# Statistics one row-maximum sooner on VectorE, and a negated mean for GpSimd's two normalizations

## What is computed

```python
x = x + attn(_layernorm(x), ctx, ctx, lengths)   # 8 heads of 16 channels; softmax(s*log(length) * q.k)
x = x + ffn(_layernorm(x), gate_w, w1, w2, w3)

def _layernorm(x, axis=-1, eps=1e-05):
    m = jnp.mean(x, axis=axis, keepdims=True)
    v = jnp.var(x, axis=axis, keepdims=True)
    return (x - m) / jnp.sqrt(v + eps)

def ffn(x, gate_w, w1, w2, w3):
    probs = softmax(x @ gate_w.T); weights, experts = top_k(probs, 2); weights /= weights.sum()
    per expert: w2 @ (silu(w1 @ x) * (w3 @ x)); the sum of the two chosen, by weight
```

## Time and profile before

| | us |
|---|---|
| median of 3 runs | 1182.57 |
| lowest and highest | 1179.75, 1184.3 |
| the profiled execution | 1178.09 |
| its span, first to last instruction | 1176.6 |

### The profile page before, as it was taken

The page is one execution under the profiler, slowest core; times in us unless marked ns, Lnnn a source line. Parts: engine busy times, 40 slices in busy tenths (PEclk is TensorE's granted clock), DMA queues, the critical chain, the costliest instruction groups (busy, mean ns, idle before and its releaser), DMA issues.

```text
span 1176.6 us, 18912 instructions
## 1 busy us (share of the span) xinstructions
PE 1033.1 (88%) x5098; PEld 413.9 (35%) x5099; DVE 683.4 (58%) x1029; ACT 427.9 (36%) x751; POOL 664.4 (56%) x571
## 2 busy tenths in 40 slices
PE   2889999999999999851899999999999999999970
PEld 0223333333333333211344444444444444444430
DVE  5867777777777777304444545455454554544355
ACT  8267777677777777741111011011111011111110
POOL 6454777777777773232386807528383483800574
PEclk9999999999999999985999999999999999999995
DMA  6575666555556544013687656738577466733678
GB/s 198 161 224 159 185 183 181 173 178 184 177 180 180 182 146 120 31 55 90 176 227 200 189 156 168 208 79 232 156 217 170 121 191 171 206 89 89 155 207 264
DMA packets 212726, 195.84 MB, mean 166 GB/s; under 512 B 137376, under 2 KB 176288, under 8 KB 207264
## 3 DMA queue, kind: packets, MB, share of 16 engines
q1 hardware_dynamic: 197760, 122.26, 40.4%
q0 software_dynamic: 14336, 71.87, 18.5%
q10 hardware_dynamic: 576, 1.05, 0.3%
HBM read 111.48 MB, written 53.00 MB: 140 GB/s over the span
## 4 chain that ended last, share of the span: by engine, by line
PE 73%; DMA 7%; DVE 7%; issue 6%; POOL 4%; ACT 1%; POOLq 1%; SPq 0%; PEldq 0%; DVEq 0%
PE rows L1162 32%; PE heads_out L1162 15%; PE heads_out L1076 7%; PE scores L1063 7%; PE rows L1049 6%; DMA W<-parts_dram 4%; DVE nm L760 4%; POOL z L527 2%; PE misc L1126 2%; PE misc L1103 1%; PE misc L1096 1%; ACT W L642 1%; DVE st L870 1%; PE misc L1118 1%; POOL zsc L526 1%
## 5 line engine op out<-in xcount | busy, mean ns | idle before, releaser
L1162 PE MATMUL rows<-W,U 128*128 (+1 forms) x1776 | 391.0, 380 | 17.8 <-DMA U<-stage 17.1
L760 DVE TENSOR_REDUCE nm<-rows 128x2 f32<-128x1024 f32 x256 | 304.3, 1215 | 100.4 <-PE rows L1049 94.0
L642 ACT ACTIVATE W<-scores 128x512 f32<-128x512 f32 x512 | 283.4, 596 | 135.9 <-PE scores L1063 135.0
L1162 PEld LDWEIGHTS rows<-W,U 128*128 128x128 bf16 x1776 | 174.0, 98 | 228.8 <-issue 21.7
L707 ACT ACTIVATE U<-rows 128x512 f32<-128x512 f32 x78 | 46.4, 597 | 509.2 <-PE rows L1162 497.0
L1162 PE MATMUL heads_out<-W,U 128*128 x888 | 197.7, 379 | 2.2 <-DVE U L889 2.2
L1049 PE MATMUL rows<-W,U 96*128 96x512 bf16 x512 | 148.8, 400 | 49.1 <-DMA W<-parts_dram 29.1
L967 DVE TENSOR_TENSOR U<-rows,U 128x512 bf16<-128x512 f32 x78 | 53.9, 691 | 230.6 <-ACT U L707 226.3
L428 POOL TENSOR_TENSOR W<-U,W 128x2048 bf16<-128x2048 f32 x42 | 171.7, 4088 | 7.7 <-POOL W L427 7.7
L1063 PE MATMUL scores<-U,W 128*128 128x512 bf16 x512 | 168.0, 385 | 5.9 <-ACT W L642 5.2
L427 POOL TENSOR_SCALAR W<-U 128x2048 bf16<-128x2048 f32 x42 | 80.8, 1924 | 146.5 <-PE rows L1162 132.8
(11 more groups left out here) (167 smaller groups left out, 723.8 us busy)
## 6 DMA issues: line engine op xcount, KB each, us to landing
U<-wpack_dram POOLq DMA_DIRECT2D x42, 1024.0 KB, 5.9
parts_dram<-U SPq DMA_DIRECT2D x32, 384.0 KB, 4.2
U<-parts_dram SPq DMA_DIRECT2D x32, 384.0 KB, 4.1
W<-parts_dram SPq DMA_DIRECT2D x32, 384.0 KB, 5.3
stage<-slots_dram SPq DMA_DIRECT2D x39, 257.0 KB, 2.9
expert_out_dram<-U SPq DMA_DIRECT2D x39, 256.0 KB
parts_dram<-U SPq DMA_DIRECT2D x32, 256.0 KB, 4.3
stage<-wpack_dram POOLq DMA_DIRECT2D x12, 512.0 KB, 5.4
```

What stands on the lines that cost most here:

```text
L642: s.activation(probs[:, w % 2, j, kk, :], sc[u % 2][:, :], ACT.Exp) \
L760: v.tensor_reduce(nm[:, bb.parity, 2 * k:2 * k + 2], p1[k % 2][:, :].rearrange("p (c k) -> p c k", c=2), AX_X, ALU.max, negate=True).then_ ...
L1162: ins = m.matmul(bank, part_of(s_part, k), W[:, bass.ds(at_w, 512)], start=(k == 0 and n == 0), stop=(k == n_chunks - 1 and n == 2))
```

## The change

VectorE's input statistics stand behind maximum 4 instead of behind maximum 5 and the reciprocal; maximum 5 and the reciprocal follow them. On GpSimd each of the two normalizations gets one more small instruction (column times -1.0, plus 0.0) that makes the negated mean, issued without a wait between it and the instruction that adds epsilon to the variance (`two`), and the pass over 512 columns adds that column where it subtracted the mean. The other edits write the same maxima in fewer calls and adjust counts.

```diff
+    def two(self, first, second):
+        first.then_inc(self.sem, 1)
+        self.done += 1
+        self.step(second)
...
-                    st.step(g.tensor_scalar(psc[:, 0:1], var, EPS, 1.0, ALU.add, ALU.mult))
+                    st.two(g.tensor_scalar(psc[:, 0:1], var, EPS, 1.0, ALU.add, ALU.mult),
+                           g.tensor_scalar(psc[:, 3:4], mean, -1.0, 0.0, ALU.mult, ALU.add))
...
-                    st.step(g.tensor_scalar(norm[:, :], xres[:, pbt.n, :], mean, psc[:, 2:3], ALU.subtract, ALU.mult))
+                    st.step(g.tensor_scalar(norm[:, :], xres[:, pbt.n, :], psc[:, 3:4], psc[:, 2:3], ALU.add, ALU.mult))
...
-                    st.step(g.tensor_scalar(zsc[:, 0:1], mv2[:, 1:2], EPS, 1.0, ALU.add, ALU.mult))
+                    st.two(g.tensor_scalar(zsc[:, 0:1], mv2[:, 1:2], EPS, 1.0, ALU.add, ALU.mult),
+                           g.tensor_scalar(zsc[:, 2:3], mv2[:, 0:1], -1.0, 0.0, ALU.mult, ALU.add))
                     st.step(g.tensor_tensor(zsc[:, 1:2], zsc[:, 0:1], mhalf[:, :], ALU.pow))
-                    st.step(g.tensor_scalar(z[:, pv.parity, 0:D], us[:, :], mv2[:, 0:1], zsc[:, 1:2], ALU.subtract, ALU.mult))
+                    st.step(g.tensor_scalar(z[:, pv.parity, 0:D], us[:, :], zsc[:, 2:3], zsc[:, 1:2], ALU.add, ALU.mult))
...
-                maxima(range(4, 6))
-                if pv.within(0, B - 1):
-                    dve.wait_ge(S["den_in"], b.n * 16)
-                    if pv.within(1, B - 1):
-                        dve.wait_ge(S["rec_out"], b.n * 16 - 16)
-                    v.reciprocal(rden[:, :], den[:, :]).then_inc(S["rec_ready"], 1)
+                maxima(range(4, 5))
                 lb = b.plus(3)
                 if lb.within(0, B - 1):
...
                     v.bn_aggr(mv1[:, lb.parity, :], st1[:, :]).then_inc(S["st1_ready"], 1)
+                maxima(range(5, 6))
+                if pv.within(0, B - 1):
+                    dve.wait_ge(S["den_in"], b.n * 16)
+                    if pv.within(1, B - 1):
+                        dve.wait_ge(S["rec_out"], b.n * 16 - 16)
+                    v.reciprocal(rden[:, :], den[:, :]).then_inc(S["rec_ready"], 1)
                 maxima(range(6, 8))
```

More of the change, by code:

```diff
@@ L17 @@
 LEAD = 4
-ENGINE_STEPS = {"prep": 8, "keys": 4, "z": 3, "route_a": 3, "route_b": 3}
+ENGINE_STEPS = {"prep": 9, "keys": 4, "z": 4, "route_a": 3, "route_b": 3}
 class Batch:
@@ L849, in slot @@
                     q_steps.end()
-                    v.nop().then_inc(S["prep_steps"], ENGINE_STEPS["prep"] - 3)
+                    v.nop().then_inc(S["prep_steps"], ENGINE_STEPS["prep"] - 4)
                     v.nop().then_inc(S["prep_done"], 1)
@@ L863, in slot @@
                         .then_inc(S["m_ready"], 1)
-                maxima(range(12, 13))
-                maxima(range(13, 14))
+                maxima(range(12, 14))
                 if pv.within(0, B - 1):
@@ L876, in slot @@
                     v.bn_aggr(mv2[:, :], st2[:, :]).then_inc(S["st2_ready"], 1)
-                maxima(range(14, 15))
-                maxima(range(15, 16))
+                maxima(range(14, 16))
                 if b.within(B, B):
```

## The result

The changed kernel takes 1162.98 us in the median of 6 runs (1159.15 to 1166.08), the kernel before 1180.26 in 6. The ratio is 0.9848, with a 95% interval from 0.9824 to 0.9873: by that ratio 17.9 us less (17.3 by the medians), where 11.3 less was forecast. The time lies 1 us under the range's lower end of 1164. The direction was right; the gain was taken too small by 6 to 7 us. Another 2.3 us of the distance to the forecast of 1171.3 come from its base, the median of three runs (1182.57), which six runs put at 1180.26.

A forecast was written before the change was run, and what follows sets the result against it. The prediction saw attention slots as a ring of waits around TensorE. It summed 6 us for VectorE's move, 4 for z and 1.3 at the attention's end: 11.3 off the 1182.57 us median gives 1171.3, range 1164 to 1184.

The forecast's parts named there:

- What bounds the kernel: TensorE fills the experts' half; an attention slot of 29.5 us is a ring of waits with no engine full.
- The three waits named: TensorE's waits in eleven slots: VectorE before rows units 7.4 us, GpSimd's z 2.5 or 6.0, the reload 3.4.
- The statistics fit into the gap, 0.67 to 0.78 us a slot: VectorE's 0.89 us of input statistics fit its 1.87 us idle before maximum 5, saving 0.67 to 0.78 us a slot.
- The reload eats part of it: 6 us instead of 9.4: Over twelve slots, late reloads cancel VectorE's gain in three and halve it in two, leaving 6 us; bounds 3 to 9.4.
- The pass at 0.62 us: GpSimd's 128x512 normalization falls from 2.08 to 0.62 us by adding instead of subtracting; held with modest trust.
- The added instruction 0.13 us: Each added 128x1 GpSimd instruction costs 0.13 us: 0.26 us of GpSimd's slot, 0.13 on the way to z.
- z is worth 4 us, near the products' idle time: z 1.33 us sooner removes TensorE's wait in fourteen slots: 3.2 to 7.7 us, taken as 4.
- The queries sooner are worth nothing directly: Queries come 2.7 us sooner on GpSimd; no direct gain, as the reload waits for scores, only room for GpSimd.
- Rival 3: The reload lands sooner because the weight load leaves before it: 16 us less, 1166 us; chance 0.08.
- rival 2: GpSimd's indirect transfers leave sooner, into the reload's flight, making it late: 7 us slower, 1189 us; chance 0.08.
- Rival 1: GpSimd's pass stays at 2.08 us and its room of 0.52 us a slot limits: 1.2 us less, 1181; chance 0.29.
- The signs named: Profile after: line 534 near 620 ns, z's wait about 13 us at the end, maximum 6 close behind, slot 28.6 us.

The follow-up runs named there:

- the VectorE part alone: Changed kernel with GpSimd's lines back to subtracting the mean, only VectorE's input statistics moved: 1173.97 us against 1179.41 for the kernel before, ratio 0.9965.
- the small load: The VectorE part alone with each of ten weight loads cut from 1024 to 64 columns (0.5 MB to 32 KB): 1172.18 us, ratio 0.9940.
- the twelve forms: Changed kernel with 24 more GpSimd passes of 128x512 behind its last work, twelve operation and operand forms, each twice: one execution, 1196.94 us.
- the GpSimd part alone: Changed kernel with VectorE's lines back in the order of before, both GpSimd passes adding the negated mean: 1171.03 us, ratio 0.9933.
- those at 0.6 and 0.7: Changed kernel with GpSimd's weight load behind the keys' first step, 1167.9 us; and with the queries' pass back to subtracting, 1165.96 us.
- the last kernel above: Changed kernel with VectorE's second statistics behind maximum 14 and z's use one score product later: 1172.19 us, ratio 0.9948.

## Why the prediction was wrong in its size

Step by step:

- **What bounds the kernel**: right. All of the gain is in the slots and at their end, and the experts' half didn't move. The three waits named were the ones that changed.
- **The statistics fit into the gap, 0.67 to 0.78 us a slot**: right, and 0.78 it is (29.02 without the move, 28.24 with it).
- **The reload eats part of it: 6 us instead of 9.4**: the first step that failed. The changed kernel's excess is 0.5 us in eleven slots, so most of what lies between 6 and the upper bound of 9.4 came through. The step held the landing of the reload fixed while GpSimd's work moved. For the VectorE part alone its reasoning holds in part: it brought 4 us, the late reloads took about 3.0 from it (the small load gives them back) and GpSimd's limit 2.3. The reading that maximum 6 starts 1.15 us after maximum 5 is over was 1.07 (296.69 less 294.40 + 1.22); nothing in the sum rests on it.
- **The pass at 0.62 us**: right in the choice between 0.62 and 2.08, and the reason given, the pair's operations, is shown by the twelve forms. It is 0.77 because two columns cost 0.15. The Trainium skill (GPSIMD Engine Reference, section 3.1) gives 1.03 cycles per element for a body with at most two operations and makes no exception for a pair with a subtraction. The estimate made from it, 0.63 us, agrees with the 0.62 us for constants without a subtraction and not with the 1.92 us of the same pass with one.
- **The added instruction 0.13 us**: it is 0.27; the 0.13 was that of two casts. With the 0.15 of the columns z came 1.04 sooner instead of 1.33, which costs 0.3 us at the end of the attention and nothing in the slots.
- **z is worth 4 us, near the products' idle time**: the second step that failed. It is 0.52 us a slot (29.53 to 29.01), 7 us in fourteen, near the 7.7 of the weight loads. This is the term that was off most. The distance between the third and the fourth score product shows why. Before:

```profile
283.49 0.39 PE L1063 MATMUL scores<-U,W 128*128 128x512 bf16 x1
284.18 0.66 PE L1096 MATMUL misc<-ident,z 128*128 128x128 f32 x4 [0.29 <-POOLq L529]
284.67 0.38 PE L1063 MATMUL scores<-U,W 128*128 128x512 bf16 x1
```

and after:

```profile
276.50 0.39 PE L1069 MATMUL scores<-U,W 128*128 128x512 bf16 x1
276.73 0.60 PE L1102 MATMUL misc<-ident,z 128*128 128x128 f32 x4
277.17 0.38 PE L1069 MATMUL scores<-U,W 128*128 128x512 bf16 x1
```

  1.18 us and 0.67: the transposes now start while the product before them is still shown as busy, so the idle time between products (0.29) is less than what the wait cost. Starts are to be compared, not ends.
- **The queries sooner are worth nothing directly**: the third step that failed, and the one that made the two parts together more than their sum. No engine waits for them in the slots, but the weight load stands behind them, and it left 1.6 us sooner by the slot's reciprocal.
- **Rival 3, the reload lands sooner as the weight load leaves before it**: this happened beside the forecast, with its 1166 near the result; it was given 8%. The reason named there was right, its sign wasn't: TensorE's wait for the reload didn't go but grew from 3.4 to 4.3 us, as the forecast had it, with the reload up to 1.2 us sooner. Its 1166 is near in part by luck, as it holds the 4 us for z. The prediction weighed it against rival 2 by a count of neighbours (the indirect transfers enter the flight, the weight load leaves it). In the slot of the earlier trace rows the indirect transfers leave 7.8 us after the reciprocal (7.5 in others) and in the changed kernel 6.4, so 1.1 to 1.4 us sooner and not 2.7, and little came late: rival 2 did not happen.
- **Rival 1's account of GpSimd's room** was right where it applies: with slow passes and the statistics moved, GpSimd is the limit at 28.91 us.
- **The signs named**: the slot is 28.24 us and not 28.6; the other signs came as said (the wait for z at the end 13.51 us, maximum 6 close behind maximum 5, line 534 at 768 ns).
- **The base**: the sum's outer end, 18 us, would have given 1162 from the six runs' 1180.26, under the result of 1163. The sizes above are what was wrong; that the time fell outside the range is also the base's 2.3 us.

With the terms as measured the sum is 9.2 for VectorE's part (0.77 x 12), 7.3 for z (0.52 x 14) and 1.0 at the end, 17.5, against 17.9 by the ratio and 15.9 in the two profiled spans, in which the stretch up to the first second statistics was 0.9 us longer after. Told apart by the traces, the fifteen distances lose 8.2 us by the GpSimd part alone and 7.7 more by VectorE's.

What stays open: which slots get a late reload. At one place of the weight load some are 1 us or more late and others not at all, and a kernel whose load leaves 1.15 us after the reciprocal (the VectorE part alone) had an excess of 2.9 us, less than those at 0.6 and 0.7 (7.7 and 4.6). Nor is it known why a slot can grow by more than its excess: that of 31.21 us is 2.3 over a clean one, with an excess of 1.1.

## What to carry to other kernels

A pass that nothing waits for can still be worth its time: ask which transfer stands behind it on its engine, and which transfer on a chain flies at that moment. A statement "moves nothing on the chain" has to be made for the transfers of that engine too. Where two parts of a change touch the same ring, measure each alone and both: here 4 and 8 us made 18. Price a wait of TensorE by the distance of the starts around it and not by the idle time between products: the wait for z was worth 0.52 us a slot, the idle time of the products said 0.29, that of the weight loads 0.59.

## What the runs showed of the hardware

On GpSimd a one-input pass of 128x512 with two operations takes 0.62 us with constants, 0.69 with one column, 0.77 with two, whatever of add and multiply it has; with a subtraction as either of the two, 1.92, 1.99 and 2.08 us. The two-input pass isn't like that: its subtraction (of a bfloat16 input) takes 1.16 us and its addition (of two float32) 1.27. And one load of 0.5 MB in flight beside a reload of 0.75 MB in two transfers made TensorE wait up to 2.0 us for the reload (2.3 in the last kernel above); with 32 KB in its place it did not wait in any of those slots.
